# Self-attentions of a two-layer decoder in steps of four heads, with four probability buffers

## What is computed

```python
# first layer, causal, 16 heads of 8 (D = 8)
att = jnp.einsum('bhqd,bhkd->bhqk', q, k) * scale
causal = jnp.tril(jnp.ones((T, T), bool))
att = jnp.where(causal[None, None], att, -jnp.inf)
y = jnp.einsum('bhqk,bhkd->bhqd', jax.nn.softmax(att, axis=-1), v)
# second layer, 16 heads of 32: softmax over all keys, the mask after it
a = jax.nn.softmax(jnp.einsum('bhsd,bhtd->bhst', q, k) * D ** (-0.5), axis=-1)
if causal:
    s, t = (a.shape[-2], a.shape[-1])
    mask = (jnp.arange(t)[None, :] > jnp.arange(s)[:, None]).astype(a.dtype)
    a = a * mask
o = jnp.einsum('bhst,bhtd->bhsd', a, v)
```

## Time and profile before

| | us |
|---|---|
| median of 3 runs | 3637.05 (3636.24 to 3638.32) |
| the profiled execution | 3659.85 |
| its span in the trace | 3658.1 |
| causal self-attention (`s2s_`), first mask matmul to last product | about 1088 to 1558 of the span |
| the other self-attention (`s5a_`) | about 2250 to 2765 of the span |

### The profile page before, as it was taken

How to read it: one execution, slowest core, us unless ns; L and a number is a source line. 1 busy time by engine, 2 the same in 40 slices (tenths; PEclk the granted TensorE clock), 3 DMA queues, 4 the chain that set the end, 5 groups by cost and what they waited for, 6 DMA issues and landing times. The chain is left out here.

```text
span 3658.1 us, 52097 instructions
## 1 busy us (share of the span) xinstructions
PE 2766.2 (76%) x15862; PEld 1904.2 (52%) x15863; DVE 2182.0 (60%) x4412; ACT 1507.2 (41%) x4235; POOL 875.8 (24%) x1280
## 2 busy tenths in 40 slices
PE   3777777641969999989335886999997699986085
PEld 2444444331956666656214754666665466654074
DVE  5999999930336666657675033787873387734044
ACT  4566566510216666545221122666662244422011
POOL 4333333425530000022103000111100122201643
PEclk7888888755979999989655587999998799986598
DMA  9100000003740000000004000000000000000166
GB/s 359 71 0 0 0 0 0 0 12 96 222 117 1 0 0 0 1 6 0 6 0 55 0 0 13 1 0 0 0 1 6 13 1 0 0 6 0 47 180 177
DMA packets 106792, 127.72 MB, mean 35 GB/s; under 512 B 30050, under 2 KB 79284, under 8 KB 102580
## 3 DMA queue, kind: packets, MB, share of 16 engines
q1 hardware_dynamic: 97460, 107.27, 9.9%
q0 software_dynamic: 9216, 19.02, 1.5%
HBM read 68.84 MB, written 57.41 MB: 35 GB/s over the span
## 5 line engine op out<-in xcount | busy, mean ns | idle before, releaser
L650 DVE TENSOR_TENSOR_SCAN s_state<-s_decay,s_state 128x4096 f32<-128x4096 f32 x32 | 276.3, 8675 | 0.0
L555 PE MATMUL s_ysumP<-s_state,ident 128*128 128x512 f32 x512 | 262.2, 656 | 0.0
L1110 ACT ACTIVATE s5a_prob<-s5a_scoreP,s5a_nmax 128x256 f32<-128x256 f32 x512 | 235.1, 475 | 41.8 <-DVE s5a_nmax L1284 41.6
L1110 ACT ACTIVATE s2s_prob<-s2s_scoreP,s2s_nmax 128x128 f32<-128x128 f32 (+1 forms) x512 | 208.3, 427 | 45.5 <-DVE s2s_nmax L1282 45.1
L462 ACT ACTIVATE s_decay<-s_delta,s_aneg 128x255 f32<-128x255 f32 x512 | 208.4, 493 | 17.7 <-DVE s_delta L626 17.6
L1284 DVE TENSOR_REDUCE s5a_nmax<-s5a_scoreP 128x4 f32<-128x1024 f32 x128 | 156.7, 1224 | 67.3 <-PE s5a_scoreP L1209 66.9
L2632 POOL DMA_INDIRECT parts<-m_y,m_to x160 | 153.1, 957 | 174.4 <-DVE m_y L2723 142.5
L1282 DVE TENSOR_REDUCE s2s_nmax<-s2s_scoreP 128x2 f32<-128x256 f32 (+1 forms) x256 | 130.8, 553 | 106.4 <-PE s2s_scoreP L1204 105.9
L2801 PE MATMUL m_turnP<-ident,m_xin 128*128 128x128 f32 x160 | 33.2, 291 | 212.6 <-DMA m_w<-in_m_w 209.5
L660 DVE TENSOR_TENSOR s_state<-s_state,s_bcP 128x1024 f32<-128x1024 f32 x128 | 147.7, 1216 | 38.3 <-PE s_bcP L502 36.7
L502 PE MATMUL s_bcP<-s_bc,s_sel 96*128 96x256 bf16 x512 | 83.9, 297 | 112.3 <-DVE s_state L660 99.3
(11 more groups left out here) (584 smaller groups left out, 6922.2 us busy)
## 6 DMA issues: line engine op xcount, KB each, us to landing
sorted<-blank SPq DMA_DIRECT2D x32, 1105.0 KB, 28.0
m_w<-in_m_w SPq DMA_DIRECT2D x120, 256.0 KB
m_xin<-sorted SPq DMA_DIRECT2D x80, 130.0 KB
m_row<-parts SPq DMA_DIRECT2D x32, 256.0 KB, 5.3
m_w<-in_m_w SPq DMA_DIRECT2D x40, 128.0 KB
s_mats<-s_scratch SPq DMA_DIRECT2D x4, 1024.0 KB, 16.2
parts<-m_y,m_to POOLq DMA_INDIRECT x160
sorted<-m_row,m_idx POOLq DMA_INDIRECT x128, 2.3
```

The source lines that it names most:

```text
L555: ins = nc.tensor.matmul(ysumP[:], ident[:], state[:, :, n, :], start=(n == 0), stop=(n == NS - 1))
L650: nc.vector.tensor_tensor_scan(cells, flat(decay[c]), cells, 0.0, ALU.mult, ALU.add).then_inc(S["scanned"], 1)
L1110: ins = nc.scalar.activation(prob[i][:, h, a:b], scoreP[i][:, h, a:b], ACT.Exp, bias=nmax[:, p % 4, h, r:r + 1], accum_out=den[s][:, r, 2 ...
```

## The change

The function goes from pairs to steps of two pairs (a "quad", four heads), four a batch. On PE the scores of both pairs are issued directly behind each other, in the order of row block first and then the four heads, so that the four row strips are used; before them the step waits for all exponentials of the quad before. Then come the transposes of the first pair of the quad before, the first item, the transposes of the second pair, the second item, the value products of both pairs behind each other, and where there is one the third item. ACT has the exponentials of both pairs with an item between them. DVE has both maxima, then (in quad 0) the reciprocals, copy-out, item, copy-out, item, then two steps of the normalization, then the third item. `prob` gets four buffers instead of two; `scoreP`, `probP` and `itemP` stay as they are, as do the number and kind of matmuls, reductions, exponentials and copies.

```diff
-        prob = [sc.sb(f"prob{i}", [P, 2, CUT]) for i in range(2)]
+        prob = [sc.sb(f"prob{i}", [P, 2, CUT]) for i in range(4)]
...
+            ITEMS = {0: [("V0", 0), ("V1", 0), ("Q1", 0)], 1: [("R0", -1), ("K1", 0), ("R1", -1)], 2: [("L", -1), ("T", 1)],
+                     3: [("Q0", 1), ("K0", 1)]}
         else:
+            ITEMS = {0: [("V0", 0), ("Q1", 0)], 1: [("R0", -1), ("K1", 0)], 2: [("L", -1), ("T", 1)], 3: [("Q0", 1), ("K0", 1)]}
...
             def exps(t, s, p):
-                wait(ac, S["turned"], n - 1)
+                wait(ac, S["turned"], n - 3)
...
-            def scores(t, s, p):
+            def scores(t, s, quad):
-                wait(pe, S["exped"], t * PAIRS + p - 1)
+                wait(pe, S["exped"], t * PAIRS + 2 * quad)
...
+                for r, (a, b) in enumerate(CUTS):
+                    for i, h in four:
...
-            def pv(t, s, p):
+            def pv(t, s, quad):
-                pe.wait_ge(S["probT_ready"], t * PAIRS + p + 1)
+                pe.wait_ge(S["probT_ready"], t * PAIRS + 2 * quad + 2)
...
             for t, s in batches(pe):
-                for p in range(PAIRS):
-                    scores(t, s, p)
-                    at(AT_A, t, s, p, make)
-                    e = earlier(t, s, p, 1)
-                    if e:
-                        turn(*e)
-                    at(AT_B, t, s, p, make)
-                    e = earlier(t, s, p, 2)
+                for quad in range(QUADS):
+                    scores(t, s, quad)
+                    e = earlier(t, s, quad, 1)
+                    for i in range(2):
+                        if e:
+                            turn(e[0], e[1], 2 * e[2] + i)
+                        item(t, s, quad, i, make)
                     if e:
                         pv(*e)
+                    item(t, s, quad, 2, make)
...
             for t, s in batches(ve):
-                for p in range(PAIRS):
-                    maxes(t, s, p)
+                for quad in range(QUADS):
+                    for i in range(2):
+                        maxes(t, s, 2 * quad + i)
...
+                    for i in range(2):
+                        if e:
+                            turn_out(e[0], e[1], 2 * e[2] + i)
+                        item(t, s, quad, i, take)
+                        if 2 * quad + i <= prep.norms and not last(t) and i == 1:
+                            prep.step(ve, st, t + 1, 2 * quad)
+                            prep.step(ve, st, t + 1, 2 * quad + 1)
+                    item(t, s, quad, 2, take)
```

More of the change, by code:

```diff
@@ L885, in attend_self @@
     PAIRS = 8
+    QUADS = 4
     WIDE = D == 32
@@ L957, in cap, with earlier, item @@
             return min(x, NB) if isinstance(x, int) else x
[L959 to L963, removed]
+        def earlier(t, s, quad, d):
+            if quad >= d:
+                return t, s, quad - d
+            return None if first(t) else (t - 1, 1 - s, quad - d + QUADS)
         if WIDE:
-            AT_A = {0: [("V0", 0)], 1: [("V1", 0)], 2: [("Q1", 0)], 3: [("K1", 0)], 4: [("L", -1)],
-                    5: [("T", 1)], 6: [("Q0", 1)], 7: [("K0", 1)]}
-            AT_B = {1: [("R0", -1)], 2: [("R1", -1)]}
-        else:
[L971 to L979, removed]
+            ITEMS = {0: [("V0", 0), ("V1", 0), ("Q1", 0)], 1: [("R0", -1), ("K1", 0), ("R1", -1)], 2: [("L", -1), ("T", 1)],
+                     3: [("Q0", 1), ("K0", 1)]}
+        else:
+            ITEMS = {0: [("V0", 0), ("Q1", 0)], 1: [("R0", -1), ("K1", 0)], 2: [("L", -1), ("T", 1)], 3: [("Q0", 1), ("K0", 1)]}
+        def item(t, s, quad, i, doing):
+            if i >= len(ITEMS[quad]):
+                return
+            n, d = ITEMS[quad][i]
+            if (d < 0 and first(t)) or (d > 0 and last(t)):
+                return
+            doing(n, t + d, s if d == 0 else 1 - s)
         loads = [(wq[:], dram[tag + "wq"]), (wk[:], dram[tag + "wk"]), (wv[:], dram[tag + "wv"]), (wo[:], dram[tag + "wo"]),
@@ L1211, in scores @@
-                ins.then_inc(S["scores"], 1)
+                for r, (a, b) in enumerate(CUTS):
+                    for i, h in four:
+                        keys = k[rows_of(i, h), quad, 0:b - a] if kind == "causal" else k[rows_of(i, h), quad, :]
+                        ins = nc.tensor.matmul(scoreP[i][:, h, a:b], q[rows_of(i, h), quad, r * P:r * P + P], keys,
+                                               start=(kind != "causal"), stop=(kind != "causal" or r == 1),
+                                               skip_group_check=(kind == "causal"))
+                        if r == 1 and h == 1:
+                            ins.then_inc(S["scores"], 1)
@@ L1324, in _ @@
                 st.begin(t)
-                for p in range(PAIRS):
-                    maxes(t, s, p)
-                    if p == 0 and not first(t):
+                for quad in range(QUADS):
+                    for i in range(2):
+                        maxes(t, s, 2 * quad + i)
+                    if quad == 0 and not first(t):
                         recip(t - 1, 1 - s)
-                    e = earlier(t, s, p, 1)
-                    if e:
-                        turn_out(*e)
-                    at(AT_A, t, s, p, take)
-                    at(AT_B, t, s, p, take)
-                    if p <= prep.norms and not last(t):
-                        prep.step(ve, st, t + 1, p)
-            turn_out(NB - 1, 1, PAIRS - 1)
+                    e = earlier(t, s, quad, 1)
+                    for i in range(2):
+                        if e:
+                            turn_out(e[0], e[1], 2 * e[2] + i)
+                        item(t, s, quad, i, take)
+                        if 2 * quad + i <= prep.norms and not last(t) and i == 1:
+                            prep.step(ve, st, t + 1, 2 * quad)
+                            prep.step(ve, st, t + 1, 2 * quad + 1)
+                    item(t, s, quad, 2, take)
+            for i in range(2):
+                turn_out(NB - 1, 1, PAIRS - 2 + i)
             recip(NB - 1, 1)
```

76 lines of the change are left out of this document (30 added, 46 removed).

## The result

The changed kernel takes 3732.7 us (median of 4 runs, 3726.1 to 3741.2) against 3636.6: ratio 1.0265, 95 per cent interval 1.0245 to 1.0285, so 96 us more. The forecast was 3828 with a range of 3665 to 3985. The profiled execution took 3741.2 (span 3739.4).

The account below looks back on a forecast made before the run. PE's work was taken to bound both stages (954 us), with DVE and ACT hidden. Chain costs of 42 us in s5a and 8 in s2s plus 141 for the clock made 3637 + 191 = 3828 us, range 3665 to 3985.

Parts of the forecast that it names:

- Four heads overlap: PE, both stages: a group for four heads lasts as long as for two; 1.84 us less a step in s5a.
- Rival C: PE strips: four heads don't run side by side as two do; 218 us more at full clock, about 3950; chance 0.09.
- PE turns from the bound into a member of a chain: Both stages: each quad becomes a round trip through the engines; 42 us more in s5a, 8 in s2s.
- the sum: Both stages' quads laid out at full clock: batches of 33.45 us in s5a and 29.3 in s2s, costing 50 us.
- Two additions on DVE: s5a: DVE free at 10.35 us after quad 0's scores start, and at 11.9 after quad 1's.
- ACT is no later: Bare quad of s5a: eight exponentials end at 6.3 us, with next scores at 7.15.
- The four `prob` buffers cost nothing and buy nothing: Both stages: no effect from four buffers, because ACT waits for `scores`, not for `prob`.
- The clock: PE, both stages: waits once a quad bring part of the time to 1.2 GHz; 141 us more.
- rival A: PE, both stages: the clock holds because waits are short and between dense groups; 3687 us; chance 0.12.
- 0.4 x 353: Clock term: a 0.4 share of time at the lower level, times 353 us for both stages if PE bounds again; 141 us.

Follow-up runs that it names:

- c1: Changed kernel with value products issued pair after pair and one full-array float32 matmul between the pairs; ratio 1.0614 to the kernel before.
- c2: Changed kernel with a quad's scores issued pair after pair and one full-array float32 matmul between the pairs; ratio 1.0361 to the kernel before.
- a2: Changed kernel with DVE's first copy-out placed between the two maxima instead of behind both; ratio 1.0094 to the kernel before.
- d1: Changed kernel with five unused 128x128 float32 matmuls on PE behind the first item of quads 0, 1 and 3; ratio 1.0290 to the kernel before.
- b3: Changed kernel with a quad's value products moved behind the scores of the quad after the next; ratio 1.0187 to the kernel before.
- b1: Changed kernel with two `prob` buffers instead of four; ratio 1.0364 to the kernel before.

## Why the prediction held, and where not

The direction and the mechanism held, the size did not: 191 us more were forecast and 96 came. The time is inside the range because the range was wide.

**Four heads overlap**: right, to 0.02 us (1.15 for 16 instructions, 1.13 for 8). The Trainium skill ("TensorE: Matmul & The Clock Gate", section "Part 3: Packing small matmuls — row/col tiling") gives 3.07 times for four row strips, measured there on 512 columns; by that the group would have lengthened by a third, an estimate, and the measurement disagrees for these matmuls. Rival C is out.

**PE turns from the bound into a member of a chain**: right, and shown by c1, c2 and a2. At full clock:

| | quad 0 | quads 1 + 2 | quad 3 | batch | more than before |
|---|---|---|---|---|---|
| s5a forecast | 8.4 | 17.9 | 7.15 | 33.45 | 2.6 |
| s5a measured | 8.65 | 18.07 | 7.41 | 34.1 | 3.3 |
| s2s forecast | 7.35 | 14.5 | 7.4 | 29.3 | 0.5 |
| s2s measured | 7.54 | 14.84 | 7.60 | 30.0 | 1.2 |

(s5a's quads 1 + 2 from d1, whose batch stayed at full clock; a clean quad of each kind from the changed kernel for the rest.) 16 x (3.3 + 1.2) = 72 us where the sum had 50. No single step makes the difference. It is 0.1 to 0.3 us a quad nearly everywhere: in quad 3 of s5a the second transposes start 4.54 us after the scores (forecast 4.46), the value products 6.52 (6.37), the next scores 7.41 (7.15). Two additions on DVE were wrong as well: 6.58 + 1.37 + 0.69 + 0.05 + 1.74 is 10.43 and not 10.35, and 7.09 + 2.74 + 0.8 + 0.8 + 0.6 is 12.03 and not 11.9. Put right and carried on they give 18.1 for quads 1 + 2 of s5a, which d1 has with 18.07. "ACT is no later" holds for the exponentials. Where K is the last item, ACT's take of it ends beside the value products or after them: in quad 3 of s2s PE waits 0.38 us for it (the row of 1366.06), where the sum had about 0.3. That is little in this order, but it is what left quads 1 and 3 as they were in b3.

**"The four `prob` buffers cost nothing and buy nothing"**: wrong. They buy 36 us (b1). I had looked at who waits in the new order and not at who would wait without them. It does not touch the sum, since the change has them.

**The clock**: right in kind (it drops all through stages that had it at 1.00 after their first batches, and rival A with 3687 is out), wrong in size. This is the term that failed: 141 us forecast, about 28 measured. In s2s d1 gives 21 us, less 2 that the kernel before also has (15 us at 1.2 GHz against d1's 9, at 0.34), so 19; in s5a the rest of the stage is 561 - 16 x 34.1 = 16 us against 501 - 16 x 30.84 = 7 before, so 9. (d1 has another batch of s5a at full clock, of 33.6; by that the chain is 64 us and the clock 36.) Both factors of 0.4 x 353 were too large. The share at 1.2 GHz is (71 + 94) / 1066 = 0.15, of which 0.03 was there before; I had given each quad the 3 us that only two in five show (49 of 126 quads, 3.4 us in the mean). And a microsecond of it costs 0.34 in s2s and 0 to 0.15 in quad 1 of s5a, where over half of that stage's lies: PE's longer work lies in front of waits, and where DVE ends the quad it is hidden. I had charged the lower level as if PE bounded the batch again, as the earlier trace rows show PE alone. The Trainium skill ("TensorE: Matmul & The Clock Gate", section "Why this matters for your kernels") warns of idle gaps longer than any in the round shown; the 1.00 of three quads fits it, the 0.82 of the fourth, whose longest PE wait is 2.80 us, does not.

The sum with the measured terms is 72 + 28 = 100 us, against 100 in the stages and 96 between the medians; that the stages agree is no test of the split, since s5a's part of the clock is their rest. The time lies 95 below the forecast: the forecast was 22 us short in the chain and 113 over in the clock, and the two errors partly cancel.

## What to carry over

A saving on the engine that bounds a stage is worth at most the distance from the old time of a step to the round trip of the new order: write the round trip of every kind of step down first, with every engine's queue in it, the slow consumers' (here ACT's takes and DVE's second maxima) above all. Put the instruction for which another engine waits ahead of the one for which nobody does yet; this one swap on DVE was worth 62 of 96 us, what it did to the clock included. Charge a lower clock only on the part of the engine's work that ends a step, and in a control experiment look in the trace whether the thing was really taken away: two of ours had changed an order and nothing else.

## What the runs showed of the hardware beyond that

- Matmuls on different strips overlap whatever their order in an uninterrupted row: 16 products as four-four or pair by pair, 0.86 and 0.88 us; 16 scores 1.15 and, by pair, as long. A single 32-wide matmul over the whole array between them adds 1.0 to 1.4 us.
- Work added to PE can shorten a stage: ten more instructions in three of four quads, whose results nobody uses, took 21 us off s2s through the clock (0.93 to 0.99), and lengthened s5a by as much. The time at 1.2 GHz can move to a neighbouring quad; what decides where, stays open.
- The longest wait of PE alone does not decide it. In the fourteen inner batches of the changed kernel eleven quads 1 of s2s stay at full clock with a wait of 2.0 to 2.35 us, while two quads 0 whose longest wait is 0.8 us have 3.4 us at 1.2 GHz; the fourteen quads 1 of s5a, with waits of 2.25 to 3.04 us, all have it.
